# A four-layer graph network on one core: shorter type sums, prompter group reports, earlier extra rows, evenly spread slabs, and steps begun in the gates

## The reference

```python
# layer 0: four steps of a gated graph network, K = 4 edge types
transformed = einsum('nd,khd->knh', feat, W) + b[:, None, :]
a = segment_sum(transformed[etypes, src], dst)
feat = gru_cell(a, feat, w_ih, w_hh, b_ih, b_hh)
# layers 1 and 2: sums over the same edges without types
# layer 3: seg_sum, seg_max, seg_mean of edge_attr (200000 x 32) by source, then an MLP
```

## Time and profile before

| | |
|---|---|
| median of 3 runs | 7337.82 us (7335.02 to 7353.33) |
| the profiled execution | 7338.52 us, its span 7336.8 us |
| sorting and clearing, to the first product of step 0 | about 1096 us |
| step 0 | 1096 to 2785 us |
| steps 1, 2, 3 (first to last matmul of the matrix product) | 2838 to 3746, 3798 to 4699, 4750 to 5639 us |
| everything after layer 0 | from about 5700 us |
| busy: PE, DVE, ACT, POOL | 67%, 60%, 51%, 51% |

### The profile page before, as it was taken

The page is one execution under the profiler, slowest core; times in us unless marked ns, Lnnn a source line. Parts: engine busy times, 40 slices in busy tenths (PEclk is TensorE's granted clock), DMA queues, the critical chain, the costliest instruction groups (busy, mean ns, idle before and its releaser), DMA issues. The chain is left out here.

```text
span 7336.8 us, 96109 instructions
## 1 busy us (share of the span) xinstructions
PE 4935.3 (67%) x39375; PEld 2538.1 (35%) x39375; DVE 4431.9 (60%) x7733; ACT 3720.7 (51%) x2634; POOL 3759.0 (51%) x3297
## 2 busy tenths in 40 slices
PE   0110238774444458999889989899988377676678
PEld 0110114432222224555545555455554211111123
DVE  9889977654334445554455545445444599999700
ACT  0000009975555455665556656566655177777401
POOL 0017777777777755688764888638870000000230
PEclk9755559987777779999999999999999576767799
DMA  9920028884443355766557756466654233334398
GB/s 412 428 73 0 0 67 277 258 229 149 158 154 145 141 198 173 239 212 221 189 173 228 241 186 231 149 224 229 224 190 142 97 143 155 153 146 158 141 418 363
DMA packets 344782, 1415.02 MB, mean 193 GB/s; under 512 B 129310, under 2 KB 182836, under 8 KB 314516
## 3 DMA queue, kind: packets, MB, share of 16 engines
q1 hardware_dynamic: 159676, 1138.67, 42.6%
q10 hardware_dynamic: 79672, 239.96, 8.7%
q0 software_dynamic: 104992, 30.24, 3.2%
HBM read 1008.21 MB, written 400.36 MB: 192 GB/s over the span
## 5 line engine op out<-in xcount | busy, mean ns | idle before, releaser
L582 PE MATMUL ps_all<-ring,T 128*64 128x448 f16 x32928 | 3324.9, 363 | 840.3 <-ACT ring L745 686.1
L582 PEld LDWEIGHTS ps_all<-ring,T 128*64 128x64 bf16 x32928 | 1923.3, 113 | 2226.1 <-issue 798.5
L744 ACT ACTIVATE ring<-ring 128x3136 uint16<-128x3136 uint8 x502 | 1410.4, 2810 | 1676.8 <-DVE t L1077 861.5
L479 POOL DMA_INDIRECT R<-in_edge_attr,eid x1568 | 1893.2, 1207 | 664.9 <-issue 477.0
L447 POOL DMA_INDIRECT mat_d<-cT,idxT x1563 | 1685.3, 1078 | 965.4 <-ACT cT L686 489.2
L745 ACT ACTIVATE ring<-ring 128x3136 uint16<-128x3136 uint8 x502 | 1405.9, 2801 | 0.0
L1115 DVE SCALAR_TENSOR_TENSOR R<-R,ring 128x784 f32<-128x784 uint16 x392 | 363.3, 974 | 811.1 <-DMA csum_d<-R 727.4
L1671 POOL DMA_INDIRECT sg<-seg_d,endI x49 | 57.8, 1179 | 1208.9 <-POOLq L199 1194.3
L536 PE MATMUL ps_all<-ident,R 128*128 128x128 f32 x448 | 108.3, 422 | 809.2 <-DVE R L835 809.2
L1614 PE MATMUL ps_all<-ad,ones 3*128 3x384 bf16 (+1 forms) x686 | 320.7, 467 | 343.4 <-ACT ps_all L1584 342.7
L1590 ACT ACTIVATE L<-ps_all,bias 128x384 f32<-128x384 f32 (+1 forms) x686 | 425.9, 621 | 148.7 <-PE ps_all L1614 145.4
(11 more groups left out here) (372 smaller groups left out, 3887.3 us busy)
## 6 DMA issues: line engine op xcount, KB each, us to landing
ring<-mat_d SPq DMA_DIRECT2D x784, 784.0 KB
C<-csum_d SPq DMA_DIRECT2D x98, 3136.0 KB, 15.5
mat_d<-ring SPq DMA_DIRECT2D x98, 1568.0 KB, 39.6
csum_d<-R ACTq DMA_DIRECT2D x196, 784.0 KB
seg_d<-R ACTq DMA_DIRECT2D x32, 1568.0 KB
msg_d<-t ACTq DMA_DIRECT2D x196, 128.0 KB
R<-in_edge_attr,eid POOLq DMA_INDIRECT x1568
mat_d<-cT,idxT POOLq DMA_INDIRECT x1563
```

Source lines behind the costliest of these rows:

```text
L479: pool.indirect_dma_start(slab[n % 2][:, c, 0:FA], None, attr, bass.IndirectOffsetOnAxis(eid[:, at:at + 1], 0)).then_inc(s_at[n % 2], 16)
L582: mm = pe.matmul(accs[h * D:(h + 1) * D, j, 0:GW], lhsT, ring[:, n % 6, h * HQ + j * GW:h * HQ + (j + 1) * GW], start=first, stop=True, sk ...
L744: act.activation(to[:, 0, :], two[:, 0, :], ACT.Copy)
```

## The change

Five things are edited. DVE's type sums are cut into instructions of half the length. POOL reports group g-1 in the middle of group g, and at the end waits once. In step 0 the extra rows come ahead of the last four blocks, and `widened_by` follows them. The turns of the slabs go by a table, 4.6 blocks apart through steps 1 to 3 (with 11 slabs no longer tied to a step), and the gathers for the extra rows are at slabs 10 and 21 (`fetch_ahead`). At the end of a step ACT widens one of the next step's first two pieces before the copies; PE makes `product(0)` once part 5 has been read out of bank 7 and `product(1)` once the message of block 0 is made; DVE makes that message between the last `before` and the last `after`; and the wait for all parts moves to the 44th pair of block 0.

```diff
-PER = 11
+PACE = 46
 def walk(st):
-    return list(range(BPS)) if st else [*range(NB - 1), NB, NB + 1, NB - 1]
+    return list(range(BPS)) if st else [*range(NB - 4), NB, NB + 1, *range(NB - 4, NB)]
-        who = "act" if n < KT * (NB - 1) or n % 2 else "dve"
+        both = n >= FIRST_OF[0, NB - 1] or FIRST_OF[0, NB] <= n < FIRST_OF[0, NB] + NX
+        who = "dve" if both and n % 2 == 0 else "act"
+def slab_turns():
+    return {FIRST + PACE * n // 10 + q: (n, q) for n in range(NS) for q in range(4)}
+SLABS = slab_turns()
+def fetch_ahead(st):
+    return next(n for n in range(2, NS + 1) if n == NS or FIRST + PACE * (n - 2) // 10 + 3 >= BPS * (st - 1) + NB - 6)
...
-            sumW = QW // 2
+            sumW = QW // 4
             def slab_of(st, c):
-                s, q = divmod(c - FIRST, 4)
-                n = PER * (st - 1) + s
-                return (n, q) if st and 0 <= s < PER and n < NS else None
+                return SLABS.get(BPS * (st - 1) + c) if st else None
...
-                    if a == 0 and g >= 4:
-                        pool.wait_ge(s_sc[(g - 4) % 8], 16 * GC * ((g - 4) // 8 + 1))
+                    if a == GC // 2 and g:
+                        pool.wait_ge(s_sc[(g - 1) % 8], 16 * GC * ((g - 1) // 8 + 1))
                         pool.sem_inc(s_done, 1)
...
-                for g in range(NGC - 4, NGC):
-                    n = sum(16 * (min(NCOL, (x + 1) * GC) - x * GC) for x in range(g % 8, g + 1, 8))
-                    pool.wait_ge(s_sc[g % 8], n)
-                    pool.sem_inc(s_done, 1)
+                last = NGC - 1
+                pool.wait_ge(s_sc[last % 8], sum(16 * (min(NCOL, (x + 1) * GC) - x * GC) for x in range(last % 8, NGC, 8)))
+                pool.sem_inc(s_done, 1)
...
-                    if n and n % PER == 0 and n // PER < STEPS - 1:
-                        gathered(n // PER)
+                    for st in range(1, STEPS - 1):
+                        if n == fetch_ahead(st):
+                            gathered(st)
...
+                                if i == 44 and c == 0 and st:
+                                    pe.wait_ge(s_h, NG * st)
                                 if i == 44 and c + 2 < NB:
...
+                def begun(st):
+                    if st:
+                        pe.wait_ge(s_tt, NG * st - 1)
+                        pe.wait_ge(s_h, NG * (st - 1) + 1)
+                    product(0, psT)
+                    pe.wait_ge(s_tc, NB * (st + 1) + 1)
+                    product(1, psT)
+                    if st:
+                        pe.wait_ge(s_tt, NG * st)
                 for st in range(STEPS):
-                    if st:
-                        pe.wait_ge(s_h, NG * st)
-                    product(0, psT)
-                    pe.wait_ge(s_tc, NB * (st + 1) + 1)
-                    product(1, psT)
+                    begun(st)
...
+                    if st + 1 < STEPS:
+                        upto(end + 2)
                     grown(st)
...
-                    quarters = [slice(o * QW, (o + 1) * QW) for o in range(NQ)]
+                    parts = [slice(o * QW // 2, (o + 1) * QW // 2) for o in range(2 * NQ)]
...
-                        for h in range(2):
+                        for h in range(4):
                             at = slice(o * QW + h * sumW, o * QW + (h + 1) * sumW)
...
                         if j + 1 < NG:
                             before(j + 1)
+                        elif st + 1 < STEPS:
+                            message(st + 1, 0)
                         after(j)
...
                     upto(piece_no(st, 0, 0))
-                    message(st, 0)
+                    if st == 0:
+                        message(st, 0)
+                    message(st, 1)
                     upto(piece_no(st, 0, KT - 1))
-                    message(st, 1)
```

More of the change, by code:

```diff
@@ L114 @@
 WIDENED = widened_by()
+def slab_turns():
+    return {FIRST + PACE * n // 10 + q: (n, q) for n in range(NS) for q in range(4)}
+SLABS = slab_turns()
+assert len(SLABS) == 4 * NS and max(SLABS) < BPS * (STEPS - 1)
+def fetch_ahead(st):
+    return next(n for n in range(2, NS + 1) if n == NS or FIRST + PACE * (n - 2) // 10 + 3 >= BPS * (st - 1) + NB - 6)
 def node_rows(tile, rows):
@@ L348, in build @@
             exC = sb(ph, "exC", [P, NX])
-            rs = sb(ph, "rs", [P, 2 * NQ])
+            rs = sb(ph, "rs", [P, 4 * NQ])
             keep = sb(ph, "keep", [P, SLAB])
@@ L1097, in added @@
                     four = [ring[:, piece_no(0, c, k) % 6, :].bitcast(U16) for k in range(KT)]
-                    quarters = [slice(o * QW, (o + 1) * QW) for o in range(NQ)]
+                    parts = [slice(o * QW // 2, (o + 1) * QW // 2) for o in range(2 * NQ)]
                     widened(dve, piece_no(0, c, 0))
                     widened(dve, piece_no(0, c, 1))
-                    for q in quarters:
+                    for q in parts:
                         ad = dve.tensor_tensor(all4[:, q], four[0][:, q], four[1][:, q], ALU.add)
@@ L1112, in added @@
                             dve.wait_ge(s_cso[o % 2], 16 * (n // 2))
-                        for h in range(2):
+                        for h in range(4):
                             at = slice(o * QW + h * sumW, o * QW + (h + 1) * sumW)
                             ad = dve.scalar_tensor_tensor(CS[o % 2][:, h * sumW:(h + 1) * sumW], all4[:, at], 1.0, four[3][:, at],
-                                                          ALU.mult, ALU.add, accum_out=rs[:, 2 * o + h:2 * o + h + 1])
+                                                          ALU.mult, ALU.add, accum_out=rs[:, 4 * o + h:4 * o + h + 1])
                         ad.then_inc(s_csm, 1)
```

## The result

The changed kernel takes 7164.24 us (median of 4 runs, 7147.41 to 7172.98) against 7345.03 us of the kernel before beside it: a ratio of 0.975, 95% interval 0.9735 to 0.9765. The kernel is faster, by 173 us between the two profiled spans (7336.8 and 7164.3). The forecast was 7104 within 7035 to 7185; its sum took 234 us off, so about 60 us were not there.

What follows compares the result with a forecast made beforehand. POOL's scatters were taken to pace step 0's later stretch, and late slabs to stall steps 1 to 3. Terms -74 + 17 - 50 - 168 + 54 - 13 = -234 us from 7338.5 gave 7104, range 7035 to 7185.

Steps and rivals of the forecast that it cites:

- the rival without relief for the scatters: Step 0: shorter type sums leave the scatters as slow as before; 7178 us, chance 0.14.
- Slabs, -168: Steps 1 to 3: with slabs 4.6 blocks apart all stalls for late slabs go, 168 us saved.
- Late slabs at the ends of steps 1 and 2, +54: Slabs 10 and 21 come behind the messages' gathers, delaying copies and gates; 54 us lost, bounds 0 and 75.
- Boundaries, -13: Three step boundaries: an earlier message and products begun during the gates save 13 us, bounds 6 and 20.
- Scatters, -74: Step 0: half-long type sums hold up POOL's scatters less; 163 us of loss falls to 89, 74 saved.
- The wait behind group 42, +17 (at most 30): Step 0, middle of group 43: POOL waits for group 42 to land; 17 us lost, bounds 0 and 30.
- Step 0's end, 37 us: From last scatter to copies, 37 us in place of 87.4; 50 us saved, bounds 35 and 55.
- POOL was not shut out: Rival: short sums shut POOL out for a whole run of sums in step 0; 7478 us, slower, chance 0.06.
- slabs did not stay the bound: Rival, steps 1 to 3: POOL needs over 82 us a slab, half the 168 us stay; 7188 us, chance 0.05.
- the late slabs did cost what was said: Rival: late slabs at the steps' ends cost little, or scatters are relieved more fully; 7050 us, chance 0.14.
- the last scatter "near 2640": Sign in the profile after: step 0's last scatter near 2640 us, where it was 2698.35.
- the 40 us to the copies: Sign in the profile after, step 0's end: 40 us from the last scatter to the copies.

Runs made afterwards that it cites:

- b2_mid: The changed kernel with the messages' gathers inside slabs 10 and 21, not ahead of them; 7141.67 us against 7348.28 for the kernel before, ratio 0.9708.
- after_again: The changed kernel as it is, run again on a slow chip; 10138.71 us against 10078.76 for the kernel before, ratio 1.0272.
- a2_reports: The kernel before with only the reports one group behind, on a slow chip; 10075.85 us against 10082.57 for the kernel before, ratio 0.9967.

## Why the prediction was right, and where its sizes were off

The largest terms came out nearly to the microsecond, but the total owes something to luck. 7164 lies in the stated range and above the forecast's own (7060 to 7150), and it is only 14 us from 7178, the rival without relief for the scatters. That rival's mechanism failed, since the scatters did get 59 us shorter; its number is near because a wait took back nearly all of that.

- **Slabs, -168: right, -171.** No pair inside steps 1 to 3 waits; "a small miss costs nothing" was not needed. That the table of slabs alone does it was not shown on a comparable chip. DVE's wait for slabs, 446 us before and 82.5 after, and that no other edit touches the turns of the slabs speak for it; the gathers themselves are no faster (1227 ns on average, 1207 before).
- **Late slabs at the ends of steps 1 and 2, +54: right.** With boundaries it is +45 against the sum's +54 - 9 = +45. b2_mid takes the cause away and the two boundaries fall by 54.2, though the steps grow by 19.
- **Boundaries, -13: right**, 4.5 each at the inner ones, as b2_mid has them, and 5.2 us from ACT's copies to step 1.
- **Scatters, -74: mechanism right, -59.** The share of the loss that stays is 105 / 163 = 0.64, where I took 0.55. The prediction had 0.6 for scatters that meet the run at any phase, and that is nearly what they do.
- **The wait behind group 42, +17 (at most 30): the mis-sized term, 47, and 53.6 with 16 small ones.** I read the old jam's end (about 1511) as a fixed time. Of the 30 us that were missing, 16 are that POOL, with shorter scatters, comes to this wait at 1477 and not at 1493.6, and 13 that the jam lasts until 1524 and not 1511, although POOL stands still meanwhile; in b2_mid the wait is 60 us. So later scatters were not what kept the jam going, and my bound of 30 us had nothing under it but one trace of a kernel that didn't wait. Why the jam grew from some 57 to 85 us is open, as is which of group 42's small transfers make it.
- **Step 0's end, 37 us: 53.5.** Three pieces are too small: from the last scatter to the first widening 14.4 us and not 8; from there to the end of the sums 33.0 and not 28.8; and ACT's early pieces, which I called off the path, put 5.9 us on it. The transfer of the sums on ACT's queue is the cause of the last, and of DVE's wait of 24.63 us; that is read from the timeline and not tried.

Added up in the trace: start of step 1 predicted 111 us sooner, in fact 45 (6 by the scatters, 34 by the end of step 0, 5 by the boundary). That is 66 us short, and the steps gave 5 us more than in the sum, which leaves the missing 60. The other rivals fell too: POOL was not shut out (scatters got shorter), slabs did not stay the bound, and the late slabs did cost what was said. The first of these has a wrong figure: by its own costs (3.5 us a block, and 160 us from 7178 to the kernel before, over 46 blocks) it would decide against the change from 7.0 us a block on, not 8.6.

Of the signs named, the last scatter "near 2640" (2692) and the 40 us to the copies (53.5) missed; the others came: scatters of 1.13 us beside sums, the wait after group 42, no idle time of PE inside the steps, and the waits for slabs 10 and 21 with none before step 3's gates.

## What to carry to other kernels

Before a wait is moved nearer to its issue on an engine that sets the pace, look for the worst landing in the trace and price the wait by that whole stretch, not by what is left of it when the engine used to arrive. When a stall is removed inside a loop, the next one sits at the loop's end, where gathers that wait for the last result stand ahead of gathers that don't: put them in the middle of the long run, as b2_mid does. Two queued things on one engine (here a transfer of sums and an early load's widening) keep their order, so "idle time" ahead of a critical copy is only free if nothing ahead of it in that queue waits. And a gain holds for the kind of chip on which it was measured: this one is 2.5% on the first and nothing on a chip like that of after_again.

## What the runs showed of the hardware

- On four of the five chips that the experiments fell on, TensorE comes down to one matmul in 2.80 us some 20 to 35 us into a slab's run of GpSimd's indirect transfers, the granted clock in the stretch 0.50 (1.2 GHz): 6.4 us of work in 32. It recovers about 5 us after the last of this slab's, and 21 to 23 us after the last scatter of step 0. DVE and ACT stand up to 21 us at a time beside the scatters of the sorting stage. It isn't so throughout: in a2_reports PE is busy 89 of 100 us beside scatters at 1600 us. On the fifth chip, that of b2_mid, PE is busy 77.00 of 77 us beside the 49 gathers of slab 2. Nothing in the traces says what ties the engines together.
- On those four chips a scatter beside no DVE work takes either 0.96 us, as in the kernel before, or 1.09 to 1.10; the means are 1.02 to 1.05 us.
- Behind group 42, where the extra rows' markers and their messages' gathers are issued together, the 16 DMA engines are at a share of 0.73 to 1.09 for over 80 us and move 26 to 96 GB/s in the changed kernel; in b2_mid it is 0.95 and 43 GB/s over 84 us.
